# Perceiver kernel on one core: the order of one transfer queue, the place of row statistics and of three norm operations

## The chip, the cores and the metric

One Trainium2 chip, and one of its cores. The program is one launch; its time is the device time of that launch in microseconds (us). The kernel before takes 2626.78 us (median of 3 runs, 2623.25 to 2628.44).

## The reference, cut to what matters

Twelve layers run one after the other on a latent `x` of 128 rows and 256 columns, beside a context `ctx` of 12544 rows and 256 columns. The change touches the first and the fourth layer, both of them cross-attention from the 128 latent rows to all context rows:

```python
# layer 0 (16 heads of 64)
kv = ctx @ w_kv; k, v = split(kv); q = layernorm(x) @ w_q
attn = softmax(q k^T / 8); out = attn v
out = relu(out @ w_out1) @ w_out2; x = x + layernorm(out) * gamma
# layer 1 (8 heads of 64): the context is normalised row by row first
xn = layernorm(ctx) * g + b
kv = concat(xn, layernorm(x)) @ Wkv; attn = softmax(mask(q k^T / 64)); x = x + layernorm((attn v) @ Wo)
```

Two things that later layers need are made on the side in layer 0: the mean and the reciprocal standard deviation of each context row (layer 1 reads them), and a sum over keys and values for the third cross-attention.

## The kernel before, in words

Every layer is a stage with its own block of engine programs. Both stages concerned use the class `ProjectedAttention`: stage `l0x` with 16 heads and `l1x` with 8. The context is cut into 14 chunks (`NCH`) of 896 rows (`CH`), a chunk into seven tiles of 128. Within a chunk the work goes by steps, one pair of heads each: `P` is 8 steps in `l0x` and 4 in `l1x`. In the code `n` is the chunk, `pr` the step in it, `m = P * n + pr`. The last chunk of `l1x` is followed by a short one for the latent rows.

A step of TensorE (`pe`) has a fixed order: keys of step m+1 (L491), scores of step m (L526), values of step m-2 (L552), value projections and, in `l0x`, side projections for a chunk (L511), and the turn of the output of step m-2 (L560). VectorE (`dve`) takes in step m: the accumulation of step m-3 (L775), the low part of the keys (L719), maximum (L736), difference (L749) and the 32x32 block transposes of the probabilities (L756), and in `l0x` statistics of the side tiles and one row statistic (`dve_row`, L995 and L997). ScalarE copies keys and values out of PSUM, takes the exponentials (L625), copies the output (L632), and at the end of its step 0 copies the next chunk's context to its high part (L596), after `normed`. GpSimd (`pool`) keeps the row sums (L872, L876), makes the low part of the context (L836, signals `c_low`) in its step 0, which begins when ScalarE's `alpha` of step 0 is there, that is late in step 1 of the others; in `l1x` it then makes the mask bias (L845), and in its step 2 the norm of the context two chunks on (L822 centre, L824 scale, L826 gain), column half by column half.

The block-transposed probabilities become fully turned ones by a round trip through memory: `sp_scatter(m)` writes 896 KB to `turns` (L409) when VectorE has signalled `blocks`, and `sp_gather(m)` reads them back as `pT` (L416) when that write has landed. TensorE's values of step m, which come in step m+2, wait for the read.

All these transfers, and those of the chunks, are issued by one engine, SyncE, in the order of its program (`sp`); a wait of one instruction holds all behind it. For each step it issues the write, then `chunk_transfer`, then the read. `chunk_transfer` holds: in step 0 the context rows of this chunk (`sp_rows`, `l0x`, L945) or, in `l1x`, mean and rstd of chunk n+2 (`sp_norm`, L442); in step 1, after a wait for `c_low` of chunk n+1, the raw context of chunk n+2 (`sp_raw`, L438; its buffer is single and `c_low` is its last reader); in step 2 the mask (`l1x`, L435); in steps 2 and 3 the save of the context's high and low part (`l0x`, L450). The raw transfer with its wait occurs for n = 0 to 11 in either stage.

Of the kernel before, what the change touches and what calls it, by code (L numbers as in the profile page):

```python
# [11 lines left out]
ALU = mybir.AluOpType  # L12
# [8 lines left out]
DC = D // 128  # L21
S2 = 12544
CH = 896
CT = CH // 128
HALF = CH // 2
NCH = S2 // CH
# [202 lines left out]
class FirstParts:  # L229
# [7 lines left out]
    def sp(self, sp):  # L237
        A = self.A
        raw, mean, rstd, weights = first_parts(A)
        sp.dma_start(raw, A["ctxT"][:, :, 0:CH]).then_inc(A["sems"]["raw_in"], 16)  # L240
        for name, dst in (("mean", mean), ("rstd", rstd)):
            sp.dma_start(dst, A["ctx_" + name][0:CH].partition_broadcast(128)).then_inc(A["sems"][name + "_in"], 16)
        for name, dst in zip(("wq", "wk", "wv"), weights):
            sp.dma_start(dst, A["L1_xattn_" + name]).then_inc(A["sems"][name + "_in"], 16)


class ProjectedAttention:
# [121 lines left out]
    def sp(self, sp):  # L369
        if self.mask_dram is not None:  # L370
            self.sp_mask(sp, 0)
        self.sp_loads(sp, 1)
        if self.side is not None:
            self.side.sp_rows(sp, 0)
        for m in range(self.P * NCH):
            n, pr = divmod(m, self.P)
            self.sp_scatter(sp, m)
            self.chunk_transfer(sp, n, pr)
            self.sp_gather(sp, m)
            if m == 0 and self.side is None:  # L380
                self.sp_out(sp)
            if m == self.P * NCH - 1 and self.side is not None:
                sp.wait_ge(self.s.sem("sum_ps"), NCH)
                self.sp_out(sp)

    def chunk_transfer(self, eng, n, pr):

        s, ahead = self.s, n + 2
        if pr == 0 and n > 0 and self.side is not None:
            self.side.sp_rows(eng, n)  # L390
        if pr == 0 and ahead < NCH and self.norm_dram is not None:
            for c in range(DC):
                eng.wait_ge(s.sem(f"scaled{c}"), ahead)
            self.sp_norm(eng, ahead)
        if pr == 1 and ahead < NCH:
            eng.wait_ge(s.sem("c_low"), 2 * ahead)
            self.sp_raw(eng, ahead)
        if pr == 2 and ahead < NCH and self.mask_dram is not None:
            eng.wait_ge(s.sem("bias"), ahead)
            self.sp_mask(eng, ahead)  # L400
        if pr in (2, 3) and ahead <= NCH and self.parts_dram is not None:
            self.sp_save(eng, n + 1, pr - 2)

    def sp_scatter(self, sp, m):

# [13 lines left out]
    def sp_loads(self, sp, n):  # L419

        s = self.s
        sp.wait_ge(s.sem("c_low"), 2 * n)
        if n < NCH:
            self.sp_raw(sp, n)
            if self.norm_dram is not None:
                self.sp_norm(sp, n)
        if self.mask_dram is not None and n < NCH:
            sp.wait_ge(s.sem("bias"), n)
            self.sp_mask(sp, n)
        if self.parts_dram is not None:  # L430
            for part in range(2):
                self.sp_save(sp, n - 1, part)
# [4 lines left out]
    def sp_raw(self, sp, n):  # L437
        sp.dma_start(self.raw[:, :, :], self.keysT_dram[:, :, n * CH:(n + 1) * CH]).then_inc(self.s.sem("raw_in"), 16)  # L438

    def sp_norm(self, sp, n):  # L440
        for name, dst, src in (("mean", self.mean, self.norm_dram[0]), ("rstd", self.rstd, self.norm_dram[1])):
            sp.dma_start(dst[:, :], src[n * CH:(n + 1) * CH].partition_broadcast(128)).then_inc(self.s.sem(name + "_in"), 16)  # L442

    def sp_out(self, sp):
        sp.dma_start(self.wo[:, :, :], self.A[self.prefix + "wo"]).then_inc(self.s.sem("wo_in"), 16)
# [366 lines left out]
            mine = slice(8 * g, 8 * g + 8)  # L812
            dve.tensor_tensor(self.acc[:, mine, :], self.acc[:, mine, :], add_cols(self.l[:, mine], self.HD), ALU.mult).then_inc(s.sem("attended"), 1)

    def norm_part(self, eng, n, c):
        s = self.s
        eng.wait_ge(s.sem("raw_in"), (n + 1) * 16)
        eng.wait_ge(s.sem("mean_in"), (n + 1) * 16)
        eng.wait_ge(s.sem("rstd_in"), (n + 1) * 16)
        eng.wait_ge(s.sem("gain_in"), 32)  # L820
        part = self.raw[:, c, :]
        eng.tensor_tensor(part, part, self.mean[:, :], ALU.subtract).then_inc(s.sem(f"centered{c}"), 1)  # L822
        eng.wait_ge(s.sem(f"centered{c}"), n + 1)
        eng.tensor_tensor(part, part, self.rstd[:, :], ALU.mult).then_inc(s.sem(f"scaled{c}"), 1)  # L824
        eng.wait_ge(s.sem(f"scaled{c}"), n + 1)
        eng.tensor_scalar(part, part, self.gain[:, 0, c:c + 1], self.gain[:, 1, c:c + 1], ALU.mult, ALU.add).then_inc(s.sem(f"normed{c}"), 1)  # L826

    def pool_norm(self, pool, n):
        for c in range(DC):
            self.norm_part(pool, n, c)  # L830

    def pool_context(self, pool, n):
        s = self.s
# [15 lines left out]
    def pool(self, pool):  # L849
        s = self.s  # L850
        if self.mask_dram is not None:
            self.pool_bias(pool, 0)
        if self.norm_dram is not None:
            self.pool_norm(pool, 1)
        if self.tail is not None:
            pool.wait_ge(s.sem("tail_high"), 1)
            pool.tensor_tensor(self.tail_parts[1][:, :, :], self.tail, self.tail_parts[0][:, :, :].bitcast(F32),
                               ALU.subtract).then_inc(s.sem("tail_low"), 1)
        if self.side is not None:
            self.side.pool_start(pool)  # L860
        if self.decay is not None:
            self.decay.pool_start(pool)
        pool.wait_ge(s.sem("cleared"), 3)
        for m in range(self.M):
            n, pr = divmod(m, self.P)
            hs, r = slice(2 * pr, 2 * pr + 2), m % self.RING
            if self.side is not None:
                self.side.pool_step(pool, n, pr)
            if self.decay is not None:
                self.decay.pool_step(pool, n, pr)  # L870
            pool.wait_ge(s.sem("alpha"), m + 1)
            pool.tensor_tensor(self.l[:, hs], self.l[:, hs], self.alpha[:, r, :], ALU.mult).then_inc(s.sem("l_scaled"), 1)  # L872
            for a in range(2):
                pool.wait_ge(s.sem(f"p{a}"), m + 1)
            pool.wait_ge(s.sem("l_scaled"), m + 1)
            pool.tensor_tensor(self.l[:, hs], self.l[:, hs], self.rs[:, r, :], ALU.add).then_inc(s.sem("l"), 1)  # L876
            if pr == 0:
                if n + 1 < NCH:
                    self.pool_context(pool, n + 1)
                if n + 1 < self.N and self.mask_dram is not None:  # L880
                    self.pool_bias(pool, n + 1)
            if pr == 2 and self.norm_dram is not None and n + 2 < NCH:
                self.pool_norm(pool, n + 2)

    def pe_outputs(self, pe, ps):
# [23 lines left out]
class ContextSide:  # L909
# [55 lines left out]
    def dve_step(self, dve, n, pr):  # L965
        if pr > 0:
            self.dve_means(dve, n, range(2 * pr - 2, min(2 * pr, CT)))
        if pr < 4:
            for t in range(2 * pr, min(2 * pr + 2, CT)):
                self.dve_moments(dve, n, t)  # L970
        if pr == 4:
            self.dve_scales(dve, n)
        if pr > 0:
            self.dve_row(dve, n, pr - 1)

    def dve_moments(self, dve, n, t):
        s = self.s
# [330 lines left out]
def stage_l1_xattn(nc, A, x, ident):  # L1308

    H = 8  # L1310
    with Stage(nc, "l1x", fast=2 * (2 * DC * CH + 2 * DC * H * 64 + H // 2 * T + 2 * CH + DC * T), held=SOON) as s:
        s.take_over(A, "raw_in", "mean_in", "rstd_in", "wq_in", "wk_in", "wv_in")
        lat, latT = s.sb("lat", [128, D]), s.sb("latT", [128, DC, T])
        pa = ProjectedAttention(s, H, A, "L1_xattn_", ident, 1.0 / 64, A["ctxT"], mask_dram=A["mask_bk1"], tail=latT[:, :, :],
                                norm_dram=(A["ctx_mean"], A["ctx_rstd"]))
# [33 lines left out]
        @block.vector  # L1349
        def _(dve):  # L1350
            link = linker(dve, s.sem("dve_steps"))
            n0.moments(dve, link, x[:, :])
            pa.norm_part(dve, 0, 0)
            n0.rescale(dve, link, lat[:, :], x[:, :])
            dve.sem_inc(s.sem("lat"), 1)
            pa.norm_part(dve, 0, 1)
            dve.wait_ge(s.sem("latT_ps"), 1)
            dve.wait_ge(s.sem("lgb_in"), 16)
            for c in range(DC):
                dve.tensor_scalar(latT[:, c, :], ps_a[:, c * 128:(c + 1) * 128], lgb[:, 0, c:c + 1], lgb[:, 1, c:c + 1],  # L1360
                                  ALU.mult, ALU.add).then_inc(s.sem("latT"), 1)
            pa.dve_first_parts(dve)
            pa.dve_clear(dve)
            pa.dve_queries(dve)
            pa.dve(dve)
            pa.dve_outputs(dve)
            dve.wait_ge(s.sem("out_ps"), 1)
            ny.dve(dve, link, y[:, :], ps_a[:, 0:D])
            dve.wait_ge(s.sem("og_in"), 16)
            link(dve.tensor_tensor(y[:, :], y[:, :], og[:, :], ALU.mult))  # L1370
            dve.wait_ge(s.sem("ob_in"), 16)
            link(dve.tensor_tensor(y[:, :], y[:, :], ob[:, :], ALU.add))
            link(dve.tensor_tensor(x[:, :], x[:, :], y[:, :], ALU.add))
# [2320 lines left out]
```

## Time and profile before

| quantity | value |
|---|---|
| median of 3 runs | 2626.78 us |
| profiled execution | 2626.45 us, span 2624.7 us, mean granted clock 0.937 |
| PE busy | 2335.8 us (89%) |
| DVE busy | 2007.8 us (76%) |
| ACT busy | 1266.9 us (48%) |
| POOL busy | 730.4 us (28%) |
| DMA | 540.96 MB, mean 206 GB/s |

PE is TensorE, DVE VectorE, ACT ScalarE, POOL GpSimd, SP SyncE; SPq marks an instruction that SyncE issues to its DMA queue. A row of the profile names the line of the kernel, the operation, what it writes and reads, and after it, in brackets, how long the engine stood idle before and who released it. Stage `l0x` lies between about 20 and 1190 us of the span, `l1x` between about 1345 and 1890 us.

### The profile page before, as it was taken

How to read it: one execution, taken by the hardware profiler on the slowest of the kernel's cores; microseconds unless marked ns; L12 is line 12 of the kernel's file. 1: busy time of each engine (PE TensorE's matmuls, PEld its weight loads, DVE VectorE, ACT ScalarE, POOL GpSimd, SP SyncE). 2: the span in 40 equal slices, each digit the busy share in tenths (PEclk: the TensorE clock that was granted, in tenths of full speed). 3: DMA queues.
4: the chain of work that ended last, by engine and by line, in shares of the span. 5: the costliest groups of instructions: out<-in, count | busy, mean ns of one | idle time of the engine just before them, and what ended most of it. 6: DMA issues, size and time to landing. Idle time of an engine off the chain costs nothing. (4 is left out here: it accounts for less than half of the span.)

```text
span 2624.7 us, 61865 instructions
## 1 busy us (share of the span) xinstructions
PE 2335.8 (89%) x23416; PEld 1876.9 (72%) x23416; DVE 2007.8 (76%) x4001; ACT 1266.9 (48%) x2509; POOL 730.4 (28%) x907
## 2 busy tenths in 40 slices
PE   8997999999999999977868989999667579999986
PEld 7886888888888888866757777777443247888873
DVE  7989899999999999975867888878652367666615
ACT  5544555555555555434645555555311264555553
POOL 1433143432443423330134545554000010010000
PEclk9999999999999999987989999999777689999996
DMA  6566556666666666556637777776377653444310
GB/s 258 204 225 220 211 204 235 238 238 241 220 217 225 239 239 227 201 186 224 218 120 267 265 263 262 259 257 241 134 306 289 252 183 118 128 142 128 88 48 23
DMA packets 179170, 540.96 MB, mean 206 GB/s; under 512 B 18012, under 2 KB 113456, under 8 KB 172736
## 3 DMA queue, kind: packets, MB, share of 16 engines
q1 hardware_dynamic: 176352, 528.52, 56.6%
q0 software_dynamic: 2304, 8.39, 0.9%
q8 instruction: 192, 3.15, 0.5%
q14 instruction: 98, 0.80, 0.1%
q10 hardware_dynamic: 224, 0.10, 0.0%
HBM read 356.76 MB, written 180.19 MB: 205 GB/s over the span
## 5 line engine op out<-in xcount | busy, mean ns | idle before, releaser
L511 PE MATMUL l0x_psum<-l0x_fast 128*128 128x512 f32 x1764 | 435.8, 399 | 1.5 <-DVE l0x_fast L713 1.0
L756 DVE STREAM_TRANSPOSE l0x_sbuf<-l0x_sbuf 128x896 f32<-128x896 f32 x224 | 388.9, 1778 | 0.6 <-issue 0.6
L511 PEld LDWEIGHTS l0x_psum<-l0x_fast 128*128 128x128 f32 x1764 | 323.1, 188 | 90.1 <-issue 22.6
L625 ACT ACTIVATE l0x_sbuf<-l0x_sbuf 128x896 f32<-128x896 f32 x224 | 234.7, 1048 | 281.3 <-DVE l0x_sbuf L736 281.3
L1808 DVE CUSTOM_DVE_ANT_0 l3x_sbuf<-l3x_psum,key_bias,l3x_sbuf 128x896 f32<-128x896 f32 x224 | 249.2, 1151 | 92.6 <-PE l3x_psum L1652 76.8
L1738 ACT ACTIVATE l3x_sbuf<-l3x_psum 128x512 f32<-128x512 f32 x392 | 221.4, 599 | 179.0 <-PE l3x_psum L1670 172.4
L491 PE MATMUL l0x_psum<-l0x_fast 128*128 128x448 f32 x1344 | 300.2, 372 | 0.0
L491 PEld LDWEIGHTS l0x_psum<-l0x_fast 128*128 128x128 f32 x1344 | 244.2, 188 | 25.0 <-DVE l0x_fast L719 0.3
L736 DVE CUSTOM_DVE_ANT_0 l0x_sbuf<-l0x_psum,l0x_sbuf 128x896 f32<-128x896 f32 x224 | 248.8, 1149 | 10.1 <-PE l0x_psum L526 10.1
L552 PE MATMUL l0x_psum<-l0x_sbuf 128*32 128x128 f32 x6272 | 204.6, 280 | 36.3 <-DVE l0x_sbuf L775 27.7
L552 PEld LDWEIGHTS l0x_psum<-l0x_sbuf 128*32 128x32 f32 x6272 | 173.5, 111 | 72.6 <-issue 61.2
L872 POOL TENSOR_TENSOR l0x_sbuf<-l0x_sbuf 128x2 f32<-128x2 f32 x112 | 21.7, 194 | 700.9 <-ACT l0x_sbuf L638 699.8
L1668 PE MATMUL l3x_psum<-l3x_fast,key_bias 128*128 128x256 f32 x784 | 207.5, 295 | 0.7 <-DVE l3x_fast L1818 0.7
L602 ACT ACTIVATE l0x_fast<-l0x_psum 128x448 fp32r<-128x448 f32 x224 | 120.3, 544 | 168.3 <-PE l0x_psum L491 168.3
L1670 PE MATMUL l3x_psum<-l3x_fast,last_keys 128*128 128x256 f32 x784 | 196.9, 281 | 0.0
L756 DVE STREAM_TRANSPOSE l1x_sbuf<-l1x_sbuf 128x896 f32<-128x896 f32 x112 | 195.6, 1784 | 0.0
L625 ACT ACTIVATE l1x_sbuf<-l1x_sbuf 128x896 f32<-128x896 f32 (+1 forms) x120 | 120.2, 1001 | 118.5 <-DVE l1x_sbuf L736 118.5
L719 DVE TENSOR_TENSOR l0x_fast<-l0x_psum,l0x_fast 128x448 fp32r<-128x448 f32 x224 | 132.9, 619 | 58.1 <-ACT l0x_fast L602 58.1
L526 PE MATMUL l0x_psum<-l0x_fast 64*128 64x448 f32 x1344 | 167.8, 381 | 0.0
L1668 PEld LDWEIGHTS l3x_psum<-l3x_fast,key_bias 128*128 128x128 f32 x784 | 149.1, 190 | 22.4 <-issue 16.9
L511 PE MATMUL l1x_psum<-l1x_fast 128*128 128x512 f32 x594 | 153.6, 406 | 5.8 <-DVE l1x_fast L719 4.0
L616 ACT ACTIVATE l0x_sbuf<-l0x_psum 128x512 f32<-128x512 f32 x196 | 114.8, 598 | 85.5 <-PE l0x_psum L511 85.2
(778 smaller groups left out, 4348.6 us busy)
## 6 DMA issues: line engine op xcount, KB each, us to landing
turns<-l0x_sbuf SPq DMA_DIRECT2D x112, 896.0 KB, 3.7
l0x_sbuf<-turns SPq DMA_DIRECT2D x112, 896.0 KB, 4.9
turns<-l1x_sbuf SPq DMA_DIRECT2D x56, 896.0 KB, 4.2
l1x_sbuf<-turns SPq DMA_DIRECT2D x56, 896.0 KB, 5.7
last_keys<-ctx_high SPq DMA_DIRECT2D x112, 224.0 KB, 3.5
ahead<-in_L_ffn_W SPq DMA_DIRECT2D x18, 1024.0 KB, 11.4
experts<-in_L_ffn_W SPq DMA_DIRECT2D x18, 1024.0 KB, 12.4
l0x_sbuf<-in_ctxT SPq DMA_DIRECT2D x14, 896.0 KB, 5.0
```

The costliest lines, as they stand in the source:

```text
L491: mm = pe.matmul(ps[:, 0:width], self.wk[w][:, c, pr * T:(pr + 1) * T], x[:, c, lo:lo + width], start=(j == 0), stop=(j == len(products) - 1))
L511: mm = pe.matmul(ps[:, :], x[:, c, t * T:(t + 1) * T], weights[w][:, c, :], start=(j == 0), stop=(j == len(products) - 1))
L526: mm = pe.matmul(self.ps_s[a][:, i, 0:width], self.q[q][half, pr, :], self.k[k][half, m % 2, lo:lo + width], start=(j == 0), stop=(j == 2))
L552: mm = pe.matmul(self.ps_o[32 * c:32 * c + 32, :].rearrange("p (i q) -> p i q", i=4), self.v[:, m // 4 % 2, t, at:at + 32], self.pT[:, m % ...
L625: act.activation(p, p, ACT.Exp, scale=-1.0, bias=self.negm[:, n % 2, 2 * pr + a:2 * pr + a + 1], accum_out=self.rs[:, m % self.RING, a:a + ...
L719: dve.tensor_tensor(self.k[1][:, m % 2, lo:lo + width], self.ps_kv[self.slot["k", m, i]][:, 0:width], self.k[0][:, m % 2, lo:lo + width].b ...
L736: dve.tensor_tensor_reduce(self.p[:, a, 0:parts * width].rearrange("p (i c) -> p i c", i=parts), self.ps_s[a][:, 0:parts, 0:width], bias.r ...
L756: dve.transpose(self.blocks[:, j, :, a * CT:(a + 1) * CT, :].rearrange("p g t c -> p t g c"), self.p[:, a, :].rearrange("p (t r g) -> p t ...
L1668: pe.matmul(ps_t[b][:, h * 2 * T:(h + 1) * 2 * T], bias[:, t * T:(t + 1) * T], eye[:, :, :].rearrange("p a t -> p (a t)"), start=True, sto ...
L1670: mm = pe.matmul(ps_t[b][:, h * 2 * T:(h + 1) * 2 * T], kst[g % 2][:, t * T:(t + 1) * T], qb[:, i % 2, :, :].rearrange("p a t -> p (a t)") ...
L1738: act.activation(p[:, u % R, :, :, :].rearrange("p h a t -> p (h a t)"), ps_t[slot["tiles", u]][:, :], ACT.Exp).then_inc(s.sem("p"), 1)
L1808: dve.tensor_tensor_reduce(junk[:, a, :].rearrange("p (i c) -> p i c", i=2), ps_s[a][:, :, 0:HALF], bias[:, n * CH:(n + 1) * CH].bitcast(F ...
```

## The change

Three things are changed, all in the two stages. On SyncE the read now comes before `chunk_transfer` in each step; the raw transfer with its wait goes from step 1 to step 0, saves from steps 2 and 3 to steps 1 and 2, the mask from step 2 to step 1, the rows of chunk n+1 are loaded at the end of chunk n; mean and rstd are two transfers with waits of their own, in steps 2 and 3, one chunk earlier than before. On GpSimd the norm goes from step 2 to step 1 and takes both halves centre by centre, then scale, then gain. On VectorE the seven row statistics of a chunk, one in each of steps 1 to 7, become two in each of steps 4, 5 and 6 and one in step 7.

```diff
         for m in range(self.P * NCH):
             n, pr = divmod(m, self.P)
             self.sp_scatter(sp, m)
+            self.sp_gather(sp, m)
             self.chunk_transfer(sp, n, pr)
-            self.sp_gather(sp, m)
...
         s, ahead = self.s, n + 2
-        if pr == 0 and n > 0 and self.side is not None:
-            self.side.sp_rows(eng, n)
-        if pr == 0 and ahead < NCH and self.norm_dram is not None:
-            for c in range(DC):
-                eng.wait_ge(s.sem(f"scaled{c}"), ahead)
-            self.sp_norm(eng, ahead)
-        if pr == 1 and ahead < NCH:
+        if pr == 0 and ahead < NCH:
             eng.wait_ge(s.sem("c_low"), 2 * ahead)
             self.sp_raw(eng, ahead)
-        if pr == 2 and ahead < NCH and self.mask_dram is not None:
+        if pr in (1, 2) and ahead <= NCH and self.parts_dram is not None:
+            self.sp_save(eng, n + 1, pr - 1)
+        if pr == self.P - 1 and n + 1 < NCH and self.side is not None:
+            self.side.sp_rows(eng, n + 1)
+        if pr == 1 and ahead < NCH and self.mask_dram is not None:
             eng.wait_ge(s.sem("bias"), ahead)
             self.sp_mask(eng, ahead)
-        if pr in (2, 3) and ahead <= NCH and self.parts_dram is not None:
-            self.sp_save(eng, n + 1, pr - 2)
+        if self.norm_dram is not None:
+            if n == 0 and pr == 0:
+                self.sp_mean(eng, ahead)
+                self.sp_rstd(eng, ahead)
+            if pr == 2 and ahead + 1 < NCH:
+                self.sp_mean(eng, ahead + 1)
+            if pr == 3 and ahead + 1 < NCH:
+                self.sp_rstd(eng, ahead + 1)
...
+    def sp_mean(self, sp, n):
+        for c in range(DC):
+            sp.wait_ge(self.s.sem(f"centered{c}"), n)
+        sp.dma_start(self.mean[:, :], self.norm_dram[0][n * CH:(n + 1) * CH].partition_broadcast(128)).then_inc(self.s.sem("mean_in"), 16)
+
+    def sp_rstd(self, sp, n):
+        for c in range(DC):
+            sp.wait_ge(self.s.sem(f"scaled{c}"), n)
+        sp.dma_start(self.rstd[:, :], self.norm_dram[1][n * CH:(n + 1) * CH].partition_broadcast(128)).then_inc(self.s.sem("rstd_in"), 16)
...
     def pool_norm(self, pool, n):
         for c in range(DC):
-            self.norm_part(pool, n, c)
+            self.norm_center(pool, n, c)
+        for c in range(DC):
+            self.norm_scale(pool, n, c)
+        for c in range(DC):
+            self.norm_gain(pool, n, c)
...
-            if pr == 2 and self.norm_dram is not None and n + 2 < NCH:
+            if pr == 1 and self.norm_dram is not None and n + 2 < NCH:
                 self.pool_norm(pool, n + 2)
...
-        if pr > 0:
-            self.dve_row(dve, n, pr - 1)
+        if pr >= 4:
+            for t in range(2 * pr - 8, min(2 * pr - 6, CT)):
+                self.dve_row(dve, n, t)
```

The functions `norm_center`, `norm_scale` and `norm_gain` are the three operations of the former `norm_part`, each with the waits it needs.

## Rows read from the trace of the kernel before

**Rows 1.** Windows: stretch, sum, then busy (instructions) by engine, PEclk, DMA share, GB/s.
```profile
520.00:600.00 80.00, 79.17 (x804) 65.06 (x803) 73.76 (x147) 41.32 (x88) 29.36 (x37) 1.00 0.64 232
1560.00:1650.00 90.00, 82.75 (x900) 66.08 (x904) 74.27 (x111) 47.34 (x101) 46.70 (x41) 1.00 0.76 272
```
**Rows 2.** Waits, whole program: who waited for whom, us in total, times, longest.
```profile
PE l1x_psum L552 <- DMA l1x_sbuf<-turns: 26.9, 19, 2.3
PE l1x_psum L560 <- ACT l1x_sbuf L632: 20.9, 29, 2.0
...
ACT l1x_fast L596 <- POOL soon L826: 26.9, 14, 4.5
```
**Rows 3.** Waits of SyncE's queue, raw transfer (L438), both stages.
```profile
SPq L438 <- POOL l0x_fast L836: 65.6, 12, 7.7
SPq L438 <- POOL l1x_fast L836: 40.1, 12, 5.0
```
**Rows 4.** Timeline of SyncE in l0x, steps 1 and 2: start, duration, instruction.
```profile
543.06 0.32 SPq L409 DMA_DIRECT2D turns<-l0x_sbuf  x1
548.65 0.56 SPq L438 DMA_DIRECT2D l0x_sbuf<-in_ctxT  x1
549.30 0.55 SPq L416 DMA_DIRECT2D l0x_sbuf<-turns  x1
...
553.07 0.32 SPq L409 DMA_DIRECT2D turns<-l0x_sbuf  x1
```
**Rows 5.** Timeline of GpSimd, same chunk of l0x: the context's low part.
```profile
544.45 4.17 POOL L836 TENSOR_TENSOR l0x_fast<-l0x_sbuf,l0x_fast 128x896 fp32r<-128x896 f32 x2
```
**Rows 6.** Timeline of TensorE in l0x: values(1) in step 3, values(3) in step 5.
```profile
557.05 1.76 PE L552 MATMUL l0x_psum<-l0x_sbuf 128*32 128x128 f32 x56
...
576.11 1.16 PE L552 MATMUL l0x_psum<-l0x_sbuf 128*32 128x128 f32 x33 [0.34 <-DVE l0x_sbuf L775]
```
**Rows 7.** Landing times: writes issued 543.1 and 553.1; reads issued 549.3 and 1607.0.
```profile
DMA to landing us min/median/max: 3.5/3.5/3.5
...
DMA to landing us min/median/max: 5.1/5.1/5.1
...
DMA to landing us min/median/max: 6.6/6.6/6.6
...
DMA to landing us min/median/max: 4.7/4.7/4.7
```
**Rows 8.** Timeline of TensorE in l0x: three values groups after waits of different length.
```profile
147.28 3.22 PE L552 MATMUL l0x_psum<-l0x_sbuf 128*32 128x128 f32 x56 [1.93 <-DMA l0x_sbuf<-turns]
...
244.58 1.76 PE L552 MATMUL l0x_psum<-l0x_sbuf 128*32 128x128 f32 x56 [2.31 <-DVE l0x_sbuf L775]
...
262.94 3.22 PE L552 MATMUL l0x_psum<-l0x_sbuf 128*32 128x128 f32 x56 [9.68 <-DVE l0x_sbuf L775]
```
**Rows 9.** Timeline of SyncE in l1x, step 1.
```profile
1629.21 0.32 SPq L409 DMA_DIRECT2D turns<-l1x_sbuf  x1
1632.72 0.56 SPq L438 DMA_DIRECT2D soon<-in_ctxT  x1
1633.38 0.55 SPq L416 DMA_DIRECT2D l1x_sbuf<-turns  x1
```
**Rows 10.** Timeline of GpSimd, same chunk of l1x: the context's low part.
```profile
1628.46 4.23 POOL L836 TENSOR_TENSOR l1x_fast<-soon,l1x_fast 128x896 fp32r<-128x896 f32 x2
```
**Rows 11.** Timeline of TensorE, same chunk of l1x: turn of step 1, values of step 3.
```profile
1626.86 0.33 PE L560 MATMUL l1x_psum<-ident,l1x_sbuf 128*128 128x128 f32 x1 [1.32 <-ACT l1x_sbuf L632]
...
1640.24 1.74 PE L552 MATMUL l1x_psum<-l1x_sbuf 128*32 128x128 f32 x56 [1.27 <-DMA l1x_sbuf<-turns]
```
**Rows 12.** Groups of VectorE: row statistics, count | busy us, mean ns | idle before.
```profile
L995 DVE BATCH_NORM_STATS2 l0x_sbuf<-l0x_sbuf 128x6 f32<-128x256 f32 x98 | 39.8, 406 | 0.0
L997 DVE BATCH_NORM_AGGREGATE l0x_sbuf<-l0x_sbuf 128x2 f32<-128x6 f32 x98 | 17.8, 182 | 3.4
```
**Rows 13.** Timeline of VectorE in l0x, step 6: the difference of the maxima.
```profile
587.17 3.67 DVE L749 TENSOR_TENSOR l0x_sbuf<-l0x_sbuf 128x2 f32<-128x2 f32 x1
```

More of the change, by code:

```diff
@@ L425, in sp_loads @@
             if self.norm_dram is not None:
-                self.sp_norm(sp, n)
+                self.sp_mean(sp, n)
+                self.sp_rstd(sp, n)
         if self.mask_dram is not None and n < NCH:
@@ L438, in sp_raw @@
         sp.dma_start(self.raw[:, :, :], self.keysT_dram[:, :, n * CH:(n + 1) * CH]).then_inc(self.s.sem("raw_in"), 16)
-    def sp_norm(self, sp, n):
-        for name, dst, src in (("mean", self.mean, self.norm_dram[0]), ("rstd", self.rstd, self.norm_dram[1])):
-            sp.dma_start(dst[:, :], src[n * CH:(n + 1) * CH].partition_broadcast(128)).then_inc(self.s.sem(name + "_in"), 16)
+    def sp_mean(self, sp, n):
[6 more added lines that the diff above has]
+        sp.dma_start(self.rstd[:, :], self.norm_dram[1][n * CH:(n + 1) * CH].partition_broadcast(128)).then_inc(self.s.sem("rstd_in"), 16)
     def sp_out(self, sp):
@@ L813, in dve, with norm_center, norm_scale, norm_gain @@
             dve.tensor_tensor(self.acc[:, mine, :], self.acc[:, mine, :], add_cols(self.l[:, mine], self.HD), ALU.mult).then_inc(s.sem("attended"), 1)
-    def norm_part(self, eng, n, c):
-        s = self.s
+    def norm_center(self, eng, n, c):
+        s, part = self.s, self.raw[:, c, :]
         eng.wait_ge(s.sem("raw_in"), (n + 1) * 16)
         eng.wait_ge(s.sem("mean_in"), (n + 1) * 16)
+        eng.tensor_tensor(part, part, self.mean[:, :], ALU.subtract).then_inc(s.sem(f"centered{c}"), 1)
+    def norm_scale(self, eng, n, c):
+        s, part = self.s, self.raw[:, c, :]
         eng.wait_ge(s.sem("rstd_in"), (n + 1) * 16)
-        eng.wait_ge(s.sem("gain_in"), 32)
-        part = self.raw[:, c, :]
-        eng.tensor_tensor(part, part, self.mean[:, :], ALU.subtract).then_inc(s.sem(f"centered{c}"), 1)
         eng.wait_ge(s.sem(f"centered{c}"), n + 1)
         eng.tensor_tensor(part, part, self.rstd[:, :], ALU.mult).then_inc(s.sem(f"scaled{c}"), 1)
+    def norm_gain(self, eng, n, c):
+        s, part = self.s, self.raw[:, c, :]
+        eng.wait_ge(s.sem("gain_in"), 32)
         eng.wait_ge(s.sem(f"scaled{c}"), n + 1)
@@ L1352, in _ @@
             n0.moments(dve, link, x[:, :])
-            pa.norm_part(dve, 0, 0)
+            pa.norm_center(dve, 0, 0)
+            pa.norm_scale(dve, 0, 0)
+            pa.norm_gain(dve, 0, 0)
             n0.rescale(dve, link, lat[:, :], x[:, :])
             dve.sem_inc(s.sem("lat"), 1)
-            pa.norm_part(dve, 0, 1)
+            pa.norm_center(dve, 0, 1)
+            pa.norm_scale(dve, 0, 1)
+            pa.norm_gain(dve, 0, 1)
             dve.wait_ge(s.sem("latT_ps"), 1)
```

## The prediction

> **What bounds the kernel now.** I read the busy time by stretch first, then the waits, then the timelines of single chunks. In a steady chunk of `l0x` TensorE is busy 79.17 of 80 us at a granted clock of 1.00, the higher level (2.4 GHz): the stage is bound by TensorE, and anything that makes it wait is added to the time. In `l1x` it is busy 82.75 of 90 us [rows 1]. What it waits for there is in two groups: values that wait for the turned probabilities (26.9 us) and turns that wait for ScalarE's output copy (20.9 us); the larger waits of the second kind start where ScalarE's context copy waits for GpSimd's norm (26.9 us) [rows 2]. In one chunk of `l1x` the two cost 1.32 and 1.27 us [rows 11]. These are the waits that the change can take away.
>
> The waits of SyncE tell what it can bring. The raw transfer waits for `c_low` in all 24 chunks that have it, 65.6 us over 12 in `l0x` and 40.1 us over 12 in `l1x`, so 5.5 and 3.3 us each [rows 3]. Before the change this wait stands behind the write of step 1, so the write is out and only the read is late: in `l0x` write 543.06, raw 548.65, read 549.30 [rows 4], and the values of step 1, in step 3 at 557.05, start without any wait [rows 6].
>
> **SyncE, step 0 and 1 of `l0x`.** The read of step 0 goes out earlier, which is worth nothing, as no wait on it is left. But the raw transfer with its wait for `c_low` now stands in step 0 behind that read, so ahead of the write of step 1. The wait ends when GpSimd has made the low part, 544.45 + 4.17 = 548.62 [rows 5], and nothing in the change makes it earlier here: raw is issued at 548.65 as before. Queued behind it on SyncE are the write and the read of step 1 and everything after. The write of step 1, ready at 543.06, goes where the read was, at 549.30: 6.24 us late [rows 4].
>
> How long it then takes: a write alone landed in 3.5 us, a read alone in 4.7, and a read issued 0.65 us behind a raw transfer in 6.6, so the raw transfer ahead costs 1.9; a write with a save issued right behind it took 5.1, so a transfer behind costs up to 1.6 [rows 7]. The write behind raw: 3.5 + 1.9 = 5.4, landed at 554.7. The read goes at 554.8 with the save and the next write right behind: between 4.7 and 6.3, I take the middle, 5.5, landed at 560.3. Values(1) want to start at 557.05 [rows 6]. TensorE waits 3.25 us, bounds 0.55 (549.30 + 3.5 + 0.1 + 4.7 = 557.6, nothing queues) and 4.05.
>
> The write of step 2, ready at 553.07 [rows 4], goes out behind read and save at about 555.7. With both ahead of it (twice 1.9, and some more as the read is long) it lands near 564.5, its read near 570; values(3) come at 576.11 [rows 6], so values(2), halfway between, near 566.6, and late by 3.25 + 1.5 they want 571.3. I take no second wait, and up to 1.5 us for the upper end.
>
> **The clock.** After waits of 1.93 and 9.68 us the next values group took 3.22 us, and after one of 2.31 us it took 1.76, the duration at full clock [rows 6, 8]; so the engine comes out of such waits at the lower of its two levels (1.2 GHz) mostly, not always. 3.22 - 1.76 = 1.46: I take 1.5 us for each of the waits forecast here, with 0 as the other bound. The Trainium skill, in "TensorE: Matmul & The Clock Gate", section "HAM oscillation — how this bites in real kernels", says that a loop which waits for a DMA between its matmuls falls back to the slow clock and starts cold each time round. By that the 1.5 would be due at every new wait, 24 times 1.5; the group after 2.31 us speaks against "each time"; without it the sum would be 36 lower.
>
> **Row statistics.** One costs 406 + 182 = 588 ns [rows 12]; 98 stay 98. Steps 1 to 3 lose one each, steps 4 to 6 gain one each. In the former TensorE does not wait for VectorE (the values at 557.05 have no wait), so nothing is gained; a reason for less than nothing is not there. After step 4 the values wait 0.34 us for VectorE's accumulation [rows 6], and the extra row is right ahead of that accumulation: 0.6 us more. What steps 5 and 6 add is met in step 6 by an instruction that is stuck for 3.67 us [rows 13] while GpSimd works, and gets free when GpSimd is done, not when VectorE arrives. So 0.6 a chunk, bounds 0 and 3 x 0.59 = 1.8.
>
> `l0x` then: 3.25 + 1.5 + 0.6 = 5.35 a chunk, times 12 = 64 us, and 0.6 for each of the two chunks without a raw transfer, 1 us. The rows' transfer at the end of a chunk, the saves a step earlier and mean and rstd cost nothing of their own: they stand behind the read and are issued in steps with room; what they add is in the 1.6 above.
>
> **`l1x`.** The norm in step 1 is done a step before ScalarE asks for it, as mean and rstd come a chunk earlier and raw lands in time: the 1.32 us goes, and what is late next on that path is nothing that the chunk shows. TensorE then wants values(1) at 1640.24 - 1.27 - 1.32 = 1637.65 [rows 11]. `c_low` is ready at 1628.46 + 4.23 = 1632.69 [rows 10]; it hangs on step 1, which gets earlier by the same 1.3, so raw goes at 1631.4 and the write of step 1 at 1632.1 (before: 1629.21 [rows 9]). It lands 5.4 later, the read goes at 1637.6, has mask and the next write behind it, 5.5: 1643.1. TensorE waits 5.45 us in place of 1.27; with the clock, 5.45 + 1.5 - 1.27 - 1.32 = 4.35 a chunk, times 12 = 52 us. Bounds: nothing queues, no clock lost, 2.75 - 2.59 = 0.15; or 6.25 + 1.5 - 2.59 and a second wait of 1.5, 6.7.
>
> **The sum.** 64 + 1 + 52 = 117 us on the profiled execution's own 2626.45 us (span 2624.7): 2744 us. That time is the median of the runs (2626.78) within 0.4 us, so it is carried over as it is.
>
> **A rule that decides.** That the write cannot pass the held raw transfer is seen in the order of rows 4: the write of 543.06 had landed by 546.6 [rows 7], and its read still went only at 549.30, right behind raw. The Trainium skill, in "DMA: Bandwidth & Descriptors", section "Anatomy of one DMA — SWDGE (gpsimd) path", says the DMA engines never wait on semaphores; the wait happens on the issuing sequencer before dispatch. By that rule the program behind the wait is held, as forecast; were waits held in the transfer alone, the second rival would come. The trace agrees: SyncE issued nothing between 543.38 and 548.65.
>
> **Rivals.**
> First: the write is late but the transfers hardly hinder one another, and the clock stays. Then the lower bounds hold: 12 x 0.55 + 12 x 0.15 = 8 us, 2635; with the clock lost in `l1x` alone 18 more, 2653. For it: DMA is busy 64 and 76% of the time only [rows 1]. Against: 6.6 against 4.7 for a read behind raw.
> Second, on the other side: the late write is hidden, and the waits of `l1x` go. It decides by one point: whether `c_low` is there before `blocks` of step 1. Then 12 x 2.59 = 31 us go, 8 come with the rows: 2604. For it: both waits are real. Against: 12 of 12 raw transfers waited in both stages [rows 3].
> Third: lateness runs on into step 4 of `l0x` and into the next chunk of `l1x`, upper bounds: (4.05 + 1.5 + 1.8 + 1.5) x 12 + 6.7 x 12 = 187, 2813. For it: writes then queue behind reads and saves. Against: about 4 us of slack in each step's round trip.
> Fourth, the change doesn't do what it says: GpSimd's norm is still late, since raw comes no earlier than before in the chunk; 12 x 1.32 = 16 more, 2760. Against: a whole step is gained.
>
> **How the numbers follow.** Forecast 0.70 (its own range 2690 to 2800), first rival 0.12, second 0.05, third 0.08, fourth 0.05. The range 2650 to 2800 leaves out most of the first, the second and the third. A measurement of this kernel can tell about 0.2% from no change, 5 us: faster 0.05 (the second), same 0.03 (the low end of the first), slower 0.92.
>
> **What would show it.** In the timeline of SyncE, raw directly followed by a write in both stages, 0.65 us apart, and the write of step 1 some 6 and 3 us behind `blocks`. In the waits, values of `l0x` waiting for `turns`, 12 times 3 us or so, and in `l1x` 12 times 5 us, each followed by a values group of over 3 us; ScalarE's wait for GpSimd's gain gone. In step 5 of `l0x` a wait of 0.9 us for L775. The forecast is wrong if the write of step 1 goes out with `blocks`, or if values(1) start without a wait.

## The result, and the profile after

The changed kernel takes 2799.83 us (median of 6 runs, 2796.13 to 2804.26), the kernel before in the same rounds 2623.06 us (2619.03 to 2628.44): a ratio of 1.0672, 95% interval 1.0654 to 1.0689. The profiled execution took 2801.14 us with a span of 2799.4, so 174.7 us more than the profiled one of before (2624.7). One of the four runs of the first experiment below took 2958.43 us at a granted clock of 0.727 (the other three at 0.933 and 0.934) and is left out of that experiment's figures.

The page of the changed kernel, busy time of each engine. Lines of the kernel have moved: the write is L413, the read L420, raw L443, the values L563, the turn of the output L571, the context's low part L856.

```profile
PE 2377.9 (85%) x23416; PEld 1908.9 (68%) x23416; DVE 2015.6 (72%) x4001; ACT 1268.8 (45%) x2509; POOL 727.4 (26%) x907
```

No engine has more instructions than before. DVE, ACT and POOL differ by 8 us at most; PE is busy 42 us longer for the same 23416 matmuls. The rest of the loss is idle time. One chunk of `l0x` in the changed kernel (columns as in [rows 1]; 88.4 us is its new length):

```profile
560.00:648.40 88.40, 81.03 (x803) 66.29 (x801) 72.97 (x147) 41.26 (x88) 29.02 (x38) 0.96 0.61 209
```

Against 80.0 us with 79.17 busy [rows 1], a chunk of `l0x` has 7.4 us of idle TensorE and 1.9 us more of busy time. The same two stages whole, first of the kernel before, then of the changed one:

```profile
20.00:1176.00 1156.00, 1113.85 (x11206) 914.31 (x11205) 1048.51 (x2074) 578.87 (x1216) 406.92 (x517) 0.99 0.62 223
1334.00:1889.00 555.00, 495.44 (x5242) 394.81 (x5243) 437.21 (x667) 285.03 (x607) 260.26 (x240) 0.97 0.69 242
```

```profile
20.00:1270.00 1250.00, 1133.96 (x11163) 928.41 (x11165) 1041.27 (x2070) 579.93 (x1215) 407.04 (x517) 0.96 0.59 206
1430.00:2064.00 634.00, 513.62 (x5240) 411.36 (x5240) 450.33 (x667) 285.26 (x607) 258.84 (x240) 0.89 0.63 212
```

The ends of the stages stand in the timeline of TensorE: the first turn for the output of `l0x` starts at 1176.33 before and at 1274.82 after, 98.5 us later; `l1x`, from its first to the same turn, takes 554.6 us before (1334.07 to 1888.65) and 634.2 after (1430.11 to 2064.29), 79.6 more. These two make 178 us; everything else together is 3 us shorter.

The waits of TensorE in the changed kernel (who waited for whom, us in total, times, longest):

```profile
PE l1x_psum L563 <- DMA l1x_sbuf<-turns: 99.7, 15, 12.9
PE l0x_psum L563 <- DMA l0x_sbuf<-turns: 78.9, 16, 7.7
PE l0x_psum L563 <- DVE l0x_sbuf L786: 32.4, 27, 9.2
...
PE l1x_psum L571 <- ACT l1x_sbuf L643: 10.3, 19, 2.0
```

and of the kernel before, beside [rows 2]:

```profile
PE l0x_psum L552 <- DVE l0x_sbuf L775: 27.7, 24, 9.7
...
PE l0x_psum L552 <- DMA l0x_sbuf<-turns: 8.4, 4, 4.3
```

So the values wait for the turned probabilities 70.5 us longer in `l0x` and 72.8 longer in `l1x`, the turns wait 10.6 us less for ScalarE's output copy, and VectorE's accumulation is waited for 4.7 us longer. With the longer busy time of the stages, 20.1 and 18.2, that is 95 us for `l0x` and 80 for `l1x`: the two differences in length are accounted for.

Now one chunk. SyncE in `l0x` of the changed kernel, end of step 0 to step 3:

```profile
584.28 0.37 SPq L420 DMA_DIRECT2D l0x_sbuf<-turns  x1
594.81 0.56 SPq L443 DMA_DIRECT2D l0x_sbuf<-in_ctxT  x1
595.46 0.55 SPq L413 DMA_DIRECT2D turns<-l0x_sbuf  x1
603.33 0.37 SPq L420 DMA_DIRECT2D l0x_sbuf<-turns  x1
603.75 0.50 SPq L461 DMA_DIRECT2D ctx_high<-l0x_fast  x1
604.34 0.42 SPq L413 DMA_DIRECT2D turns<-l0x_sbuf  x1
613.67 0.36 SPq L420 DMA_DIRECT2D l0x_sbuf<-turns  x1
```

After the read of step 0 SyncE issues nothing for ten microseconds, since raw waits for GpSimd. The two events that matter here are VectorE's block transposes of step 1, which the write waits for, and GpSimd's low part of the context, which raw waits for:

```profile
585.74 3.45 DVE L767 STREAM_TRANSPOSE l0x_sbuf<-l0x_sbuf 128x896 f32<-128x896 f32 x2
```

```profile
590.61 4.18 POOL L856 TENSOR_TENSOR l0x_fast<-l0x_sbuf,l0x_fast 128x896 fp32r<-128x896 f32 x2
```

The write of step 1 could have gone at 585.74 + 3.45 = 589.19; raw is let go by 590.61 + 4.18 = 594.79, and the write follows at 595.46, 6.27 us late. TensorE in the same steps, with the values of step 1 and, two steps on, of step 3:

```profile
609.32 3.21 PE L563 MATMUL l0x_psum<-l0x_sbuf 128*32 128x128 f32 x56 [6.04 <-DMA l0x_sbuf<-turns]
...
619.95 1.77 PE L563 MATMUL l0x_psum<-l0x_sbuf 128*32 128x128 f32 x56
...
630.88 1.76 PE L563 MATMUL l0x_psum<-l0x_sbuf 128*32 128x128 f32 x56 [0.84 <-DVE l0x_sbuf L786]
```

The first is the wait that was 0 in [rows 6]; values(2) at 619.95 have none; the third is the accumulation wait of 0.34 in [rows 6]. And `l1x`, SyncE and then TensorE:

```profile
1734.13 0.56 SPq L443 DMA_DIRECT2D soon<-in_ctxT  x1
1734.79 0.54 SPq L413 DMA_DIRECT2D turns<-l1x_sbuf  x1
1742.60 0.37 SPq L420 DMA_DIRECT2D l1x_sbuf<-turns  x1
```

```profile
1728.39 0.27 PE L571 MATMUL l1x_psum<-ident,l1x_sbuf 128*128 128x128 f32 x1
...
1747.71 3.21 PE L563 MATMUL l1x_psum<-l1x_sbuf 128*32 128x128 f32 x56 [7.32 <-DMA l1x_sbuf<-turns]
```

The turn in front of the wait no longer waits for ScalarE (1.32 us in [rows 11]), and the 1.27 us of the values there has become 7.32.

### The profile page after: what moved, and what is told of

It is laid out like the page before. It is cut to its first block and busy times, and to the rows that moved or that the text cites. A ratio compares the mean times of both kernels' runs of the same rounds, so it can differ in the third digit from the quotient of the medians.

```text
span 2799.4 us, 61907 instructions
## 1 busy us (share of the span) xinstructions
PE 2377.9 (85%) x23416; PEld 1908.9 (68%) x23416; DVE 2015.6 (72%) x4001; ACT 1268.8 (45%) x2509; POOL 727.4 (26%) x907
## 5 line engine op out<-in xcount | busy, mean ns | idle before, releaser
L522 PE MATMUL l0x_psum<-l0x_fast 128*128 128x512 f32 x1764 | 441.7, 403 | 1.4 <-DVE l0x_fast L724 1.0
L563 PE MATMUL l0x_psum<-l0x_sbuf 128*32 128x128 f32 x6272 | 220.3, 294 | 111.4 <-DMA l0x_sbuf<-turns 78.9
L563 PEld LDWEIGHTS l0x_psum<-l0x_sbuf 128*32 128x32 f32 x6272 | 184.7, 117 | 151.3 <-DMA l0x_sbuf<-turns 88.3
L892 POOL TENSOR_TENSOR l0x_sbuf<-l0x_sbuf 128x2 f32<-128x2 f32 x112 | 21.7, 194 | 796.9 <-ACT l0x_sbuf L649 795.8
L563 PE MATMUL l1x_psum<-l1x_sbuf 128*32 128x128 f32 x3168 | 119.6, 311 | 100.6 <-DMA l1x_sbuf<-turns 99.7
L563 PEld LDWEIGHTS l1x_psum<-l1x_sbuf 128*32 128x32 f32 x3168 | 98.2, 125 | 122.6 <-DMA l1x_sbuf<-turns 106.6
```

Source lines behind the costliest of these rows:

```text
L522: mm = pe.matmul(ps[:, :], x[:, c, t * T:(t + 1) * T], weights[w][:, c, :], start=(j == 0), stop=(j == len(products) - 1))
L563: mm = pe.matmul(self.ps_o[32 * c:32 * c + 32, :].rearrange("p (i q) -> p i q", i=4), self.v[:, m // 4 % 2, t, at:at + 32], self.pT[:, m % ...
```

## The experiments

Each was compared with the kernel before on its own chip. Stage lengths are measured as above, `l0x` from the start of the span (before 1176.3, after 1274.8) and `l1x` from its first turn (before 554.6, after 634.2). The theory at the outset: raw's wait for `c_low`, in front of the write of step 1, makes nearly all of the loss. Rivals: the order "read, then transfers" does it, or the rows, or the norm.

**Raw with its wait back in step 1, behind the read; all else as changed.**

```diff
-        if pr == 0 and ahead < NCH:
+        if pr == 1 and ahead < NCH:
             eng.wait_ge(s.sem("c_low"), 2 * ahead)
             self.sp_raw(eng, ahead)
```

> The changed kernel with one edit: the raw transfer and its wait for c_low go back to step 1, behind that step's read. Theory (the held write of step 1 makes the loss): no values group of either stage waits for turns over 2 us any more, the 24 waits of 6 and 7.4 us and the slow groups after them go, and what is left of the change is its gain in l1x (2.6 a chunk) and its loss by rows (0.5 a chunk): 2626 - 31 + 7 = 2602, between 2590 and 2620. Rival (the new order, with transfers queued behind each read and in front of the next write, makes the loss): the raw transfer is then still in front of the write of step 2, and the time stays above 2700.

Measured: 2643.16 us (median of three runs), ratio 1.0078 (1.0054 to 1.0101). That is 21.7 us above the kernel before on its chip (2621.47), where the changed kernel is 176.8 above: 155 us are gone by moving two lines by one step; `l0x` is at 1182.3, six above before. The expectation of 2602, below the kernel before, is missed by 41 us: `l1x` takes 571.7, 17 above before. Its SyncE there, from behind the read of one step (1498.16) to that of the next:

```profile
1498.62 0.46 SPq L448 DMA_DIRECT2D soon<-ctx_mean  x1
1499.19 0.36 SPq L413 DMA_DIRECT2D turns<-l1x_sbuf  x1
1507.40 0.37 SPq L420 DMA_DIRECT2D l1x_sbuf<-turns  x1
```

Behind three of the four reads of a chunk stands a transfer, and the next write comes right behind both: here it lands in 8.2 us (its read follows at 1507.40). So the order has a price of its own, which the experiment on the order below measures.

**A second raw buffer in `l1x` alone, so that its raw transfer has no wait to hold the queue with; `l0x` is that of the changed kernel.**

```diff
+        self.raws = [self.raw, self.raw if norm_dram is None else s.sb("raw_odd", [128, DC, CH])]
...
-            eng.wait_ge(s.sem("c_low"), 2 * ahead)
+            eng.wait_ge(s.sem("c_low"), 2 * ahead if self.norm_dram is None else 2 * ahead - 2)
```

> The changed kernel with a second buffer for the raw context in l1x alone, so that in step 0 of l1x the raw transfer waits for c_low of the chunk before, which is long there; its place in the queue is that of the changed kernel, and l0x is left as it is. Theory (the wait holds the write): the waits of l1x of 7.4 us with the 1.5 of the clock after each go, 12 x 8.9 = 107 less than the changed kernel: 2693, between 2680 and 2710; l0x keeps its 12 waits of 6. Rival (place and order in the queue, not the wait): l1x keeps waits of over 4 us, time above 2750.

Measured: 2728.94, ratio 1.0408 (1.0389 to 1.0427). `l1x` falls from 634.2 to 557.7 while its raw load still goes out in step 0 with the same bytes; `l0x` keeps its waits (5.5 to 7.2, one of 3.3) and its length (1273.5). The writes of `l1x` behind raw still land slowly, in 6.4 to 9.6 us, but they are no longer held: one goes at 1612.66, when its block transposes end (1609.15 + 3.48). So the slow landing without the lateness costs some ten microseconds (557.7 beside the 547.1 that `l1x` takes with the norm alone, below); the held write is needed for most of the loss. The time lies 36 us above the expectation: `l1x` comes back to its length of before and not below it, since waits of up to 4.5 us for the turned probabilities stay, 40.3 us in all.

**The wait left in step 0, raw itself issued in step 1 behind the read.**

```diff
         if pr == 0 and ahead < NCH:
             eng.wait_ge(s.sem("c_low"), 2 * ahead)
+        if pr == 1 and ahead < NCH:
             self.sp_raw(eng, ahead)
```

> The changed kernel, the wait for c_low left in step 0, the raw transfer itself issued in step 1 behind that step's read: the write is held, but nothing is queued ahead of it. Theory (of the loss, the hold is the smaller part and the transfer ahead of the write the larger, 4.3 us of its landing): the write of step 1 lands in 3.5 to 3.7 us in place of 7.8; values(1) wait 0 to 2 us in l0x and 2 to 4 in l1x; 2650 to 2690. Rival (the hold alone makes it): waits as before, 2780 to 2800.

Measured: 2756.26, one run. Neither of the two expected: the loss goes to the next step. SyncE and TensorE of `l0x`:

```profile
581.71 0.32 SPq L414 DMA_DIRECT2D turns<-l0x_sbuf  x1
585.26 0.37 SPq L421 DMA_DIRECT2D l0x_sbuf<-turns  x1
585.68 0.56 SPq L444 DMA_DIRECT2D l0x_sbuf<-in_ctxT  x1
...
586.98 0.62 SPq L414 DMA_DIRECT2D turns<-l0x_sbuf  x1
598.76 0.36 SPq L421 DMA_DIRECT2D l0x_sbuf<-turns  x1
```

```profile
590.12 1.76 PE L564 MATMUL l0x_psum<-l0x_sbuf 128*32 128x128 f32 x56
604.67 3.00 PE L564 MATMUL l0x_psum<-l0x_sbuf 128*32 128x128 f32 x56 [5.84 <-DMA l0x_sbuf<-turns]
```

The held write of step 1, with no load in front, lands in 3.5 us as before (585.26 - 581.71), and values(1) at 590.12 do not wait, though the write went 5.6 us after its block transposes (572.62 + 3.46). The write of step 2, only 0.9 us late (582.63 + 3.46), stands behind a read, raw and a save, and its read goes 11.8 us after it; values(2) wait 5.84. In `l0x` lateness of the write alone is hidden; a landing of 11.8 us is not. In `l1x` values(1) still wait 2.0 to 2.7 us in ten of the chunks.

**Raw cut in two: one column half in step 0 behind the wait, the other in step 1 behind the read.**

```diff
         if pr == 0 and ahead < NCH:
             eng.wait_ge(s.sem("c_low"), 2 * ahead)
-            self.sp_raw(eng, ahead)
+            self.sp_half(eng, ahead, 0, "raw_in")
+        if pr == 1 and ahead < NCH:
+            self.sp_half(eng, ahead, 1, "raw_late")
```

> The changed kernel, the raw transfer cut in two: the first column half (448 KB) in its place in step 0, the second in step 1 behind that step's read. If the price of the transfer ahead goes by its bytes, the write of step 1 lands in about 5.6 us in place of 7.8, the waits fall by 2.1 each, 24 x 2.1 = 52: 2748. If it is a fixed price of a write behind a load, the write still takes over 7 us and the time stays at 2790 to 2800.

Measured: 2760.39, one run, between the two, nearer to the price by bytes. SyncE of `l0x`:

```profile
584.10 0.33 SPq L448 DMA_DIRECT2D l0x_sbuf<-in_ctxT  x1
584.52 0.38 SPq L415 DMA_DIRECT2D turns<-l0x_sbuf  x1
590.22 0.37 SPq L422 DMA_DIRECT2D l0x_sbuf<-turns  x1
```

Behind half a load the write lands in 5.7 us (590.22 - 584.52); behind a whole one in 7.8; alone in 3.5 [rows 7]. So 2.2 us for 448 KB and 4.3 for 896: with these two sizes it goes by bytes. Over the 22 writes that stand right behind the load, the half costs them 5.5 to 6.8 us here and the whole 7.5 to 9.5 in the changed kernel. The other half then stands in front of the write of step 2, where values(2) wait 2.47, which the estimate by bytes did not contain.

**The pair exchanged: wait still in step 0, raw directly behind the held write of step 1 instead of ahead of it.**

```diff
         if pr == 0 and ahead < NCH:
             eng.wait_ge(s.sem("c_low"), 2 * ahead)
-            self.sp_raw(eng, ahead)
...
             self.sp_scatter(sp, m)
+            if pr == 1 and n + 2 < NCH:
+                self.sp_raw(sp, n + 2)
             self.sp_gather(sp, m)
```

> The changed kernel, wait for c_low left in step 0, the raw transfer directly behind the held write of step 1 in place of directly ahead of it: the pair swapped, nothing else. Theory (what is ahead of a write costs it 4.3 us, what is behind costs 1.6, and a read behind a load 1.9): write lands in 3.5 to 5.1 in place of 7.8, the read in 5 to 6.6; values(1) wait 1 to 3 us in l0x in place of 6, 3 to 5 in l1x in place of 7.4; 2700 to 2740. Rival (bytes in flight count, not their order): waits as in the changed kernel, over 2780.

Measured: 2688.05, one run: 112 us below the changed kernel, with the same wait at the same place. SyncE and TensorE of `l0x`:

```profile
560.57 0.32 SPq L414 DMA_DIRECT2D turns<-l0x_sbuf  x1
560.94 0.56 SPq L444 DMA_DIRECT2D l0x_sbuf<-in_ctxT  x1
564.70 0.38 SPq L421 DMA_DIRECT2D l0x_sbuf<-turns  x1
```

```profile
571.26 1.76 PE L564 MATMUL l0x_psum<-l0x_sbuf 128*32 128x128 f32 x56 [2.24 <-DMA l0x_sbuf<-turns]
```

The write lands in 4.1 us with raw behind it (4.1 to 4.3 in 23 of the 24 chunks), against 7.8 with raw ahead; the wait falls from 6.04 to 2.24 and the group after it runs at 1.76 instead of 3.21. (Values(2), ten microseconds on, wait 1.46 and run at 1.76 too. In other chunks values(1) took 2.53, 2.94 and 3.21 after waits of 2.06, 2.16 and 2.65.) It comes out 12 us below the range expected. Together with the first run: of the 155 us of raw's place, 112 hang on which of the two transfers is first, and 43 (64.7 us above the kernel before, against 21.7) on the rest, the held write and raw in front of its read.

**The norm alone: the kernel before with GpSimd's norm in step 1, its three operations in their order of before.**

```diff
-            if pr == 2 and self.norm_dram is not None and n + 2 < NCH:
+            if pr == 1 and self.norm_dram is not None and n + 2 < NCH:
                 self.pool_norm(pool, n + 2)
```

> The kernel before with one part of the change alone: GpSimd makes the norm of l1x in step 1 (one edit). The order of SyncE's queue and the rows are those of before. Theory (the norm was late, and its place is worth the wait of ScalarE): the turns of step 1 in l1x no longer wait 1.3 us for ScalarE, ScalarE's context copy no longer for the gain; 11 x 1.32 = 15 us: 2608, between 2602 and 2614. Rival (the wait only moves on, to the values that wait for turns a step later): 2618 to 2626, with waits for turns longer by the same amount.

Measured: 2609.16, ratio 0.9949 (0.993 to 0.9967): 14 us of gain, as expected. The turns' wait for ScalarE falls from 20.9 us over 29 [rows 2] to 10.1 over 17; the wait for the turned probabilities (26.9 before) is 28.1.

**The rows alone: the kernel before with two row statistics in each of steps 4 to 6.**

```diff
-        if pr > 0:
-            self.dve_row(dve, n, pr - 1)
+        if pr >= 4:
+            for t in range(2 * pr - 8, min(2 * pr - 6, CT)):
+                self.dve_row(dve, n, t)
```

> The kernel before with the row statistics in steps 4 to 7 alone. Theory (an extra row right ahead of the accumulation in step 4 is 0.5 us a chunk): 14 x 0.5 = 7 us slower, 2629 to 2631 beside 2623; the wait for the accumulation in step 5 of l0x 0.85 in place of 0.34. Rival (rows are hidden or even help the steps they leave): within 2 us of before.

Measured: 2629.66, ratio 1.0023 (1.0012 to 1.0034): 6 us of loss, as expected. TensorE's wait for VectorE's accumulation in `l0x` rises from 27.7 to 32.3 us, nearly what it is in the changed kernel (32.4).

**The order alone: the kernel before with the read ahead of the chunk's transfers, each in its step of before.**

```diff
             self.sp_scatter(sp, m)
-            self.chunk_transfer(sp, n, pr)
             self.sp_gather(sp, m)
+            self.chunk_transfer(sp, n, pr)
```

> The kernel before with the read of each step put in front of chunk_transfer, all transfers in their steps of before. Theory (a transfer that stood ahead of the read now stands ahead of the next write, and a write behind another transfer is the one that loses most): in l0x, where a step is 10 us and the queue runs empty between, nothing, 1176 us to the first output product as before; in l1x the writes behind a read and a transfer land in 6 to 9 us in place of 3.6 and values wait 2 to 5 us for turns in most chunks: 15 to 40 us slower. Rival (a read that goes out at once is a gain): 10 to 20 us faster.

Measured: 2641.79, ratio 1.0071 (1.0052 to 1.0091): 18 us of loss, all of it in `l1x` (570.7 against 554.6; `l0x` 1177.3 against 1176.3). SyncE there:

```profile
1608.92 0.55 SPq L438 DMA_DIRECT2D soon<-in_ctxT  x1
1609.56 0.55 SPq L409 DMA_DIRECT2D turns<-l1x_sbuf  x1
1618.81 0.37 SPq L416 DMA_DIRECT2D l1x_sbuf<-turns  x1
```

Raw no longer holds up the read of its step, but it stands between that read and the next write, which now takes 9.25 us to its read. In the order of before raw stood between a write and its own read: the write had a head start there, and the read paid 1.9 us.

**Norm in step 1 and the mask of `l1x` in step 3, on the kernel before.**

```diff
-        if pr == 2 and ahead < NCH and self.mask_dram is not None:
+        if pr == 3 and ahead < NCH and self.mask_dram is not None:
```

> The kernel before with the norm in step 1, as in the run of the norm alone (2609.16, ratio 0.9949), and with l1x's mask transfer moved from step 2 to step 3. Theory now held (what stands directly behind a read or write on SyncE's queue lengthens its landing): the read of step 1, issued right behind raw, loses the mask behind it, the waits of values(1) in l1x (12 of 1.0 to 1.8 us, 3.7 once) get some 0.5 us shorter each, and in step 3 nothing waits that did not: about 6 us less than the norm alone, 2603 (2599 to 2607). Rival (only the raw load is large enough to matter, the small mask does not): no change against the norm alone, 2609, same waits. Second rival: the mask's later landing holds GpSimd's bias and so its context in the next chunk, raw goes later: over 2612.

Measured: 2604.53, ratio 0.993 (0.9911 to 0.9949). It beats the kernel before by 0.7% and the changed one by about 7%. The time lies in the range expected (2599 to 2607), but whether the mask's place has a part in it is not settled: the interval overlaps that of the norm alone, and in its profile the waits for the turned probabilities fall only from 28.1 to 23.0 us.

The waits of steady chunks stay at 1.0 to 1.8 us: they did not become shorter by 0.5 each, as expected. What fell were three of 2.5 to 2.7 us in early chunks, to 1.1 and 1.2.

## Why the prediction was right or wrong

The forecast was 2744 us, the measured time 2799.83, 0.2 us inside the upper end of the range. Sign, place and mechanism are as forecast; the loss is 177 us in place of 117. That it still lies inside is luck: in both stages the single wait is longer than its upper bound, and the second waits for which the range had room did not come. By its steps:

**SyncE held in step 0: right.** Raw is followed by the write 0.65 us later in both stages, the write is 6.27 us late in the chunk shown (forecast 6.24), and values(1) wait in all 24 chunks. Moving raw by one step takes back 155 us. SyncE's raw transfer now waits longer, since nothing goes out before it: 137.3 us in `l0x` and 95.9 in `l1x`, 12 times each, against 65.6 and 40.1 [rows 3]. Of the 112 writes of `l0x`, 75 still wait for VectorE (112 before); the others are ready and stand behind something.

**How long the write takes: the step that failed.** The prediction took 3.5 + 1.9 = 5.4 us for the write behind raw, with the 1.9 from a read behind raw [rows 7]. It landed in 7.8, 4.3 more than alone. Over all writes of `l1x` the median rose from 4.2 to 7.9 us. The read then took 5.9 in place of 5.5. So in `l0x` the wait is 3.25 + 2.4 + 0.4 = 6.05, against 6.04 in the chunk shown and 6.0 on average over the 12 (72.0 us; 3.83 to 7.66). In `l1x` the write is 2.4 longer and the read, 5.1 us from its issue to the values, 0.4 shorter: 5.45 + 2.0 = 7.45, against a mean of 7.5 over 11 chunks. The upper bounds of 4.05 and 6.25 kept the same 5.4 for the write, and so were too low as well.

The trace of before could have told it. There is a write in it that stands 0.67 us behind a read of 896 KB, a transfer in the direction of a load, and it took 7.2 us (another, 0.82 us behind, took 7.0; the read goes when the write has landed):

```profile
1532.29 0.37 SPq L416 DMA_DIRECT2D l1x_sbuf<-turns  x1
1532.96 0.32 SPq L409 DMA_DIRECT2D turns<-l1x_sbuf  x1
1540.20 0.37 SPq L416 DMA_DIRECT2D l1x_sbuf<-turns  x1
```

The 1.9 came from a read behind a load instead. The other price taken from [rows 7], up to 1.6 us for a transfer behind, was misread: the write at 553.07, which took 5.1, also stood 3.77 us behind a read. The write of the next step has the same kind of save 0.38 us behind it, nothing in the 4.9 us ahead, and its read goes after 3.6:

```profile
563.10 0.33 SPq L409 DMA_DIRECT2D turns<-l0x_sbuf  x1
563.48 0.43 SPq L450 DMA_DIRECT2D ctx_low<-l0x_fast  x1
566.72 0.36 SPq L416 DMA_DIRECT2D l0x_sbuf<-turns  x1
```

The exchanged pair shows what the mis-sized term is worth: the same held write with the load behind it gives back 112 us. But the term does not carry the loss alone. If the write goes out with its block transposes and write and read land as fast as alone (3.5 + 0.1 + 4.7 = 8.3), the values have time to spare: 5.8 us in the chunk of `l0x` shown (609.32 - 6.04 - 589.19 - 8.3), 2.2 in that of `l1x` (1747.71 - 7.32 - 1729.85 - 8.3, with the block transposes there at 1726.37 + 3.48 and the write 4.94 us late). Lateness uses it up, and every microsecond of landing beyond that is waited for: 6.27 + 4.3 + 1.2 - 5.8 = 6.0 in `l0x`, 4.94 + 4.3 + 0.4 - 2.2 = 7.4 in `l1x`. By the same sums each alone is hidden in `l0x`, or nearly so, and leaves 2.5 to 2.7 us in `l1x`. The run with the wait left in step 0 agrees (no wait in the chunk of `l0x` shown, 2.0 to 2.7 in `l1x`), and so does that with the second raw buffer in the main (2.37 behind the write of 1612.66, 4.5 at most).

**The first chunk of `l1x`: not foreseen.** There values(1) waited 12.9 us. SyncE issues four transfers in front of the write of step 1: raw, mean and rstd (left out), and the output weights (L456):

```profile
1468.61 0.55 SPq L443 DMA_DIRECT2D soon<-in_ctxT  x1
...
1470.33 0.65 SPq L456 DMA_DIRECT2D l1x_sbuf<-in_L_xattn_wo  x1
1471.03 0.47 SPq L413 DMA_DIRECT2D turns<-l1x_sbuf  x1
1482.38 0.37 SPq L420 DMA_DIRECT2D l1x_sbuf<-turns  x1
```

The write takes 11.35 us to its read, 7.85 more than alone. That is 5 us beyond the other chunks, once.

**No second wait in step 4: right** in the chunk shown (619.95). In the other chunks of `l0x` values(2) wait 0.27 us at most, and once values(3) wait 1.73. The write of step 2 did go behind read and save and took 9.3 us, but the 4 us of slack, and the wait just made, cover it.

**The clock: right.** The values group after the wait took 3.10 to 3.22 us in 23 of the 24 chunks (2.92 in one), against 1.76 at full clock [rows 8]; the two stages are busy 20.1 and 18.2 us longer for the same work, against 18 and 18 forecast. The Trainium skill's rule on loops that wait for a DMA ("TensorE: Matmul & The Clock Gate", section "HAM oscillation — how this bites in real kernels") agrees with these rows. It is not so after every wait: in the exchanged pair the group after 2.24 us of waiting took 1.76.

**The rows: right.** The wait for the accumulation went from 0.34 to 0.84 us, 0.5 against 0.6 forecast, and the change alone costs 6 us.

**The norm: right.** The turn's 1.32 us is gone, and the change alone brings 14 us, against 1.32 x 12 = 16. The fourth rival falls with it. In the changed kernel this gain is there and covered by the new wait.

**"Cost nothing of their own": wrong by some 18 us alone.** The saves, mask, mean and rstd behind the read were costed at nothing since the read no longer stands behind them. What they stand in front of is the next write, and the forecast looked at that for step 2 of `l0x` alone. In `l1x` nothing covers it: the order alone costs 16 us there. This hardly shows in the changed kernel, where the wait of step 1 comes last anyway; it shows as soon as raw is moved back, and it is why that version is slower than the kernel before.

**The rivals.** The first (transfers hardly hinder one another, lower bounds) is excluded by 7.8 against 3.5; the second (write hidden) by `c_low` coming 5.6 us after `blocks`. The third had the right size, 2813, by the wrong way: lateness does not run on, the single wait is longer.

**The sum.** `l0x`: 12 waits of 6.0, 12 x 1.5 for the clock, 5 for the rows, 95 against 98.5 measured. `l1x`: 11 x 7.5 + 12.9 = 95, and 18 for the clock, less the former waits, 26.9 and 10.6: 76 against 79.6. Together 171 of 177. What is left open is why a write suffers more behind a load (4.3) than a read does (1.9); the runs show the size and that it goes with the bytes, not the cause.

## What to carry to other kernels

On a queue that is issued in order, price a moved transfer by what comes to stand behind it, at each of its neighbours, and in the direction of that neighbour: a row of a read behind a load does not price a write behind a load. Look for a row in which the same kind of transfer stands as close behind the same kind; the trace of before had one. A transfer with a wait belongs behind the last thing that is urgent at that point; here that is between a write and its own read, where the write has a head start and the queue would be idle for its landing anyway. When parts of a change have opposite signs, run each alone: here a norm moved by one step is worth 14 us and was buried under a loss of more than ten times that.

## What the runs showed of the hardware that was not expected

A write of 896 KB to memory landed in 3.5 us alone, in 3.6 with a save and in 4.1 with a load of 896 KB issued 0.4 us behind it, in 5.7 behind a 448 KB load, in 7.8 behind an 896 KB load, and in 9.3 behind a read of 896 KB and a save. How close it stands counts too, but not alone: in the kernel before, writes took 7.2 us when issued 0.67 us behind a read, 6.0 at 1.51, 3.6 at 6.53, but 4.8 in one case and 7.5 in another at 2.3. The load that stood ahead of it landed in 6.3 us (4.9 before): so both lose by it, and the one behind loses most. A read behind the same load took 6.6 in place of 4.7.

After waits of 2.24 and 1.46 us the next values group ran at 1.76 us, the higher of the two clock levels; after one of 1.93 it had taken 3.22 [rows 8]. The length of a wait alone does not say at which level TensorE comes out of it.
